# Building the transposed one-hot on VectorE from receivers spread over 64 partitions

## What is computed

```python
h   = relu(layernorm(x))
cat = concatenate((h[src], h[dst], edge_attr), axis=-1)
msg = relu(cat @ W1 + b1)
aggr = segment_sum(msg, dst, num_segments=12500)
out = x + layernorm(aggr + h, gamma, beta)
```

## Time and profile before

| what | us |
|---|---|
| median of three executions | 2785.59 |
| lowest and highest of them | 2776.02, 2791.99 |
| span of the profiled execution | 1998.5 |
| mean granted TensorE clock in it | 0.922 |
| own time of the profiled execution | not given |
| first to last gather of the main stage | 77.9 to 1983.7 |

### The profile page before, as it was taken

The page is one execution under the profiler, slowest core; times in us unless marked ns, Lnnn a source line. Parts: engine busy times, 40 slices in busy tenths (PEclk is TensorE's granted clock), DMA queues, the critical chain, the costliest instruction groups (busy, mean ns, idle before and its releaser), DMA issues.

```text
span 1998.5 us, 51574 instructions
## 1 busy us (share of the span) xinstructions
PE 1675.0 (84%) x13397; PEld 1619.2 (81%) x13397; DVE 847.0 (42%) x2958; ACT 832.9 (42%) x1853; POOL 1501.5 (75%) x1579
## 2 busy tenths in 40 slices
PE   5788889888897888888798788888888888888886
PEld 5688888788887887888787788887888778878786
DVE  7534444444344443444444343343333344334434
ACT  5544444444444444444443343343343334334333
POOL 7777777777777777777777777777777777777775
PEclk9798988898899899899899998999899899999988
DMA  9544444444444444454444444444444444444442
GB/s 267 164 126 120 125 123 125 122 135 114 131 123 122 120 132 125 114 138 121 122 135 111 123 129 117 114 128 122 113 130 115 120 118 130 116 123 125 110 129 74
DMA packets 208223, 252.43 MB, mean 126 GB/s; under 512 B 43789, under 2 KB 132341, under 8 KB 208197
## 3 DMA queue, kind: packets, MB, share of 16 engines
q1 hardware_dynamic: 136756, 139.76, 23.9%
q0 software_dynamic: 50048, 102.60, 20.6%
q10 hardware_dynamic: 21392, 9.77, 1.7%
HBM read 229.38 MB, written 22.59 MB: 126 GB/s over the span
## 4 chain that ended last, share of the span: by engine, by line
POOL 37%; issue 25%; DMA 16%; PE 14%; DVEq 4%; DVE 2%; POOLq 1%; ACT 0%; ACTq 0%; SPq 0%
POOL a_rows L523 34%; DMA a_rows<-table_a,picks 15%; PE ps_pre L683 4%; PE ps_pre L684 4%; DVEq L1209 3%; POOL aggr L486 2%; PE ps_edge L664 2%; PE ps_hot L671 2%; PE ps_sum L694 1%; PE ps_fin L694 1%; DVE msg L1205 1%; POOLq L530 0%; PE ps_sum L701 0%; DVEq L1202 0%; DVE e_norm L1237 0%
## 5 line engine op out<-in xcount | busy, mean ns | idle before, releaser
L523 POOL DMA_INDIRECT a_rows<-table_a,picks x1516 | 1445.1, 953 | 464.5 <-issue 417.8
L906 ACT ACTIVATE msg<-msg 128x512 f32<-128x512 f32 x391 | 246.4, 630 | 1037.8 <-DVE msg L1205 1029.6
L1205 DVE TENSOR_TENSOR msg<-ps_pre,a_rows 128x512 f32<-128x512 f32 x391 | 270.5, 692 | 927.5 <-DMA a_rows<-table_a,picks 643.4
L683 PE MATMUL ps_pre<-w_c,edge_cols 128*128 128x128 f32 x3128 | 650.9, 292 | 0.0
L684 PE MATMUL ps_pre<-b_win,onehot_cols 128*128 128x128 f32 x3128 | 645.3, 290 | 0.0
L683 PEld LDWEIGHTS ps_pre<-w_c,edge_cols 128*128 128x128 f32 x3128 | 522.3, 210 | 0.0
L684 PEld LDWEIGHTS ps_pre<-b_win,onehot_cols 128*128 128x128 f32 x3128 | 517.8, 208 | 0.0
L671 PE MATMUL ps_hot<-ident,onehot 128*128 128x128 f32 x1564 | 262.7, 295 | 11.2 <-DVE onehot L1186 11.2
L694 PE MATMUL ps_sum<-onehot,msg 128*128 128x64 f32 x1568 | 207.3, 276 | 72.4 <-ACT msg L906 69.0
L694 PEld LDWEIGHTS ps_sum<-onehot,msg 128*128 128x128 f32 x1568 | 196.6, 197 | 82.6 <-ACT msg L906 78.4
L664 PE MATMUL ps_edge<-ident,edges 128*128 128x128 f32 x1564 | 259.0, 292 | 1.5 <-ACT dst_f L819 1.4
(11 more groups left out here) (123 smaller groups left out, 1062.8 us busy)
## 6 DMA issues: line engine op xcount, KB each, us to landing
edges<-in_edge_attr SPq DMA_DIRECT2D x391, 256.0 KB
a_rows<-table_a,picks POOLq DMA_INDIRECT x1516
b_win<-table_b SPq DMA_DIRECT2D x391, 32.0 KB
out<-out_rows SPq DMA_DIRECT2D x97, 64.0 KB
table_b<-b_rows ACTq DMA_DIRECT2D x96, 64.0 KB
x_all<-in_x SPq DMA_DIRECT2D x13, 448.0 KB, 5.8
table_a<-a_out SPq DMA_DIRECT2D x13, 448.0 KB, 4.0
table_early<-e_rows ACTq DMA_DIRECT2D x48, 64.0 KB
```

Of the source, the lines that this page charges most:

```text
L523: pool.indirect_dma_start(a_rows[:, u, k, :], None, table_a[:, :], bass.IndirectOffsetOnAxis(ap=picks[:, u, k:k + 1], axis=0),).then_inc(s ...
L683: pe.matmul(to, edge_cols[:, u % 2, k * P:(k + 1) * P], w_c[:, :], start=True, stop=False)
L906: act.activation(msg[:, u % 2, :, :], msg[:, u % 2, :, :], ACT.Relu).then_inc(s_msg, 1)
L1205: dve.tensor_tensor(msg[:, u % 2, :, :].rearrange("p k f -> p (k f)"), ps_pre[u % 2][:, :], a_rows[:, u, :, :].rearrange("p k f -> p (k f) ...
```

## The change

The one-hot with nodes on the partitions is no longer made by transposing. SyncE loads the 512 receivers of the group, as int32, to each of 64 partitions (`dst_win`, a DMA that reads the same 2 KB of `dst` 64 times). VectorE (`hot_columns`) compares them with base + partition number, held as one column of `base_all`, and writes fp32 ones and zeros to `onehot_cols[0:64]`. Its input is read with a step of four words, since edge p*4+k belongs at column k*128+p. The four transposes of the one-hot on TensorE and the eviction on ScalarE go. The product with the window has 64 rows of contraction where it had 128, so the unused rows need no zeros and three memsets go. `count` (for `one_hot`) and the zero (for `clear`) are read from PSUM, in the bank that the transposes used. `dst_win` shares its place with buffers of the first stage, so SyncE starts the main stage when all of `table_a` is stored.

```diff
+        space = sb("space", [P, 4 * CHUNK * H])
+        dst_win = space[0:WIN, 0:UNROLL * GROUP].bitcast(I32).rearrange("w (u e) -> w u e", u=UNROLL)
...
+        ps_count, ps_zero = ps_hot[0][:, 0:WIN], ps_hot[0][:, WIN:WIN + 1]
...
                     if past(i, 1):
                         sp.wait_ge(s_edge_turned, g - UNROLL + 1)
+                        sp.wait_ge(s_hot_cols, g - UNROLL + 1)
                     sp.dma_start(edges[:, u, :], group_rows(start_of(i, u))).then_inc(s_edges[u], 16)
+                    start = start_of(i, u)
+                    sp.dma_start(dst_win[:, u, :],
+                                 dst[bass.ds(start, GROUP)].rearrange("(o e) -> o e", o=1).to_broadcast([WIN, GROUP])
+                                 ).then_inc(s_dst_win[u], 16)
...
-                sp.wait_ge(s_zero, 1)
+                for par in range(2):
+                    sp.wait_ge(s_a_stored[par], (CHUNKS // 2) * 16)
+                sp.wait_ge(s_b_first, 1)
...
+            pool.iota(part[:, :], pattern=[[0, 1]], base=0, channel_multiplier=1,
...
-                    pe.wait_ge(s_hot, g + 1)
-                    if past(g, 2):
-                        pe.wait_ge(s_hot_cols, g - 1)
-                    for k in range(SUB):
-                        mm = pe.transpose(ps_hot[u % 2][:, k * P:(k + 1) * P], onehot[:, u, k, :], ident[:, :])
-                    mm.then_inc(s_hot_turned, 1)
...
-                        mm = pe.matmul(to, onehot_cols[:, u % 2, k * P:(k + 1) * P], b_win[:, u, :],
+                        mm = pe.matmul(to, onehot_cols[0:WIN, u % 2, k * P:(k + 1) * P], b_win[0:WIN, u, :],
...
-                    act.wait_ge(s_hot_turned, g + 1)
-                    act.activation(onehot_cols[:, u % 2, :], ps_hot[u % 2][:, :], ACT.Copy).then_inc(s_hot_cols, 1)
...
-            dve.memset(zeros[:, :], 0.0)
-            dve.memset(b_win[:, :, :], 0.0)
-            dve.memset(onehot[:, :, :, :], 0.0).then_inc(s_zero, 1)
...
-                        count[:, 0:WIN].unsqueeze(1).to_broadcast([P, SUB, WIN]),
+                        ps_count.unsqueeze(1).to_broadcast([P, SUB, WIN]),
...
+                def hot_columns(i, u):
+                    g = i * UNROLL + u
+                    dve.wait_ge(s_dst_win[u], (i + 1) * 16)
+                    if past(g, 2):
+                        dve.wait_ge(s_pre, g - 1)
+                    dve.tensor_scalar(onehot_cols[0:WIN, u % 2, :].rearrange("w (k p) -> w k p", k=SUB),
+                                      dst_win[:, u, :].rearrange("w (p k) -> w k p", k=SUB),
+                                      base_all[0:WIN, bass.ds(g, 1)], None, ALU.is_equal).then_inc(s_hot_cols, 1)
...
-                    dve.tensor_copy(aggr[:, bass.ds((j + AHEAD) * P, P)], zeros[:, :])
+                    dve.tensor_copy(aggr[:, bass.ds((j + AHEAD) * P, P)], ps_zero.to_broadcast([P, P]))
...
                             one_hot(*after(i, u, 2))
+                        if not (last and u == groups - 1):
+                            hot_columns(*after(i, u, 1))
```

More of the change, by code:

```diff
@@ L106, in build @@
         ones = sb("ones", [P, P])
-        zeros = sb("zeros", [P, P])
+        part = sb("part", [P, 1])
         eps = sb("eps", [P, 1])
@@ L116, in build @@
         flag = sb("flag", [1, 1], I32)
-        centred = sb("centred", [P, 2, CHUNK, H])
+        space = sb("space", [P, 4 * CHUNK * H])
+        centred = space[:, 0:2 * CHUNK * H].rearrange("p (a b f) -> p a b f", a=2, b=CHUNK)
+        h_cols = space[:, 2 * CHUNK * H:].rearrange("p (a b n) -> p a b n", a=2, b=CHUNK)
+        dst_win = space[0:WIN, 0:UNROLL * GROUP].bitcast(I32).rearrange("w (u e) -> w u e", u=UNROLL)
         mean_all = sb("mean_all", [P, BLOCKS])
-        h_cols = sb("h_cols", [P, 2, CHUNK, P])
         a_out = sb("a_out", [P, 2, CHUNK, H])
@@ L219, in build @@
         s_b_stored = sem("s_b_stored")
-        s_zero = sem("s_zero")
         s_gate_pool = sem("s_gate_pool")
@@ L231, in build @@
         s_edge_turned = sem("s_edge_turned")
-        s_hot_turned = sem("s_hot_turned")
+        s_dst_win = [sem(f"s_dst_win{u}") for u in range(UNROLL)]
+        s_count_kept = sem("s_count_kept")
         s_edge_cols = sem("s_edge_cols")
@@ L473, in _ @@
                       allow_small_or_imprecise_dtypes=True).then_inc(s_const, 1)
+            pool.iota(part[:, :], pattern=[[0, 1]], base=0, channel_multiplier=1,
+                      allow_small_or_imprecise_dtypes=True).then_inc(s_const, 1)
             pool.memset(eps[:, :], EPS).then_inc(s_const, 1)
-            pool.wait_ge(s_const, 4)
+            pool.wait_ge(s_const, 5)
             pool.affine_select(out=ident[:, :], in_=ident[:, :], compare_op=ALU.not_equal, fill=1.0,
@@ L563, in _ @@
         def _(pe):
-            pe.wait_ge(s_const, 5)
+            pe.wait_ge(s_const, 6)
             def turn_ids(a, q):
@@ L689, in sums @@
                     g = i * UNROLL + u
+                    pe.wait_ge(s_hot, g + 1)
                     pe.wait_ge(s_msg, g + 1)
@@ L780, in _ @@
         def _(act):
-            act.wait_ge(s_const, 5)
+            act.wait_ge(s_const, 6)
             def deviate_chunk(c):
@@ L1097, in _ @@
             ins.then_inc(s_range, 1)
-            dve.wait_ge(s_const, 5)
+            dve.wait_ge(s_const, 6)
             dve.wait_ge(s_range, 2)
@@ L1123, in _ @@
             crooked = dve.value_load(flag[0:1, 0:1], min_val=0, max_val=ID_ROWS)
-            dve.wait_ge(s_zero, 1)
             dve.wait_ge(s_pad, 2)
@@ L1272, in _ @@
                 mask()
+                dve.tensor_copy(ps_count, count[:, 0:WIN])
+                dve.memset(ps_zero, 0.0).then_inc(s_count_kept, 1)
                 dve.tensor_tensor(dst_f[:, :, :], dst_f[:, :, :],
@@ L1278, in _ @@
                 dve.wait_ge(s_rel, 2)
+                dve.tensor_scalar(base_all[:, :], base_all[:, :], part[:, 0:1], None, ALU.add).then_inc(s_rel, 1)
+                dve.wait_ge(s_count_kept, 1)
                 one_hot(0, 0)
                 one_hot(0, 1)
+                dve.wait_ge(s_rel, 3)
+                hot_columns(0, 0)
                 def rounds(s, early):
```

## The result

| | before | changed |
|---|---|---|
| median of four executions, us | 2782.5 | 3455.2 |
| lowest and highest | 2776.0, 2792.0 | 3401.9, 3467.6 |

The ratio is 1.2297 with an interval of 1.2228 to 1.2366: 23% slower. The direction was the forecast one, the size lies 540 us above the upper end of the range. The profiled execution of the changed kernel took 3443.98 us and its span is 3442.2 us, so here nothing lies outside the instructions.

What follows compares the result with a forecast made beforehand. The prediction took the gathers' pace on GpSimd, 1.249 us each, as the bound. Terms -14.0 + 40.2 + 20.1 = +46.3 us on 2785.6 gave 2831.9 us, some 1.7% slower, range 2757 to 2915.

Steps and rivals of the forecast that it cites:

- The product with the window has 64 rows: TensorE's product with the window of `table_b`: contraction over 64 rows instead of 128, given no cost in the sum.
- The cover that the prediction named for TensorE: TensorE's work per group hides behind the gathers' pace unless a group costs it over 4.87 us.
- TensorE's savings worth nothing: Removing 262.7 us of TensorE transposes and 229.5 us of ScalarE evictions gains nothing, as the gathers set the pace.
- The hold of the gathers: `hot_columns` on VectorE delays GpSimd's gathers: 40.2 us at their start plus 20.1 us past their middle.
- 20.1 forecast: Delay at a gather's second critical moment, somewhat past its middle: half of the range from nothing to a full 40.2 us.
- H: Part of `hot_columns` in which data stream, put at 507 ns; bounds 271 and 1014 ns.
- the prediction's formula: Gather delay per VectorE instruction at one critical moment: H x H/(2P), with P the gathers' pace of 1249 ns.
- the first moment: Critical moment at a gather's start, where `hot_columns` was to cost 102.9 ns x 391 = 40.2 us.
- The 14.0 us for `one_hot` and `clear`: Gathers' excess over their median, saved by moving the second input of `one_hot` to PSUM: minus 14.0 us, bounds 0 and minus 20.1.
- A constant outside the instructions: The 787.1 us by which the profiled span falls short of the median time stay unchanged; called the weakest premise.
- executions without the profiler are bound otherwise: Rival: loop really lasts 2786 us, TensorE binding at its lower clock; at least 262.7 us come off, 2523 us; chance 0.11.
- Landings, SyncE's queue, the tail: Added receiver loads of 51 MB may land some tenths late, within four groups of slack: nothing; the tail stays.

Runs made afterwards that it cites:

- session 1: Follow-up runs timed together, the unchanged kernel before taking 2000.15 us; the kernel before with only the 64-row product took 2216.5 us, ratio 1.1105.
- session 5: Last follow-up runs timed together, the kernel before taking 2817.9 us; the kernel before with only the 64-row product took 3079.1 us, ratio 1.0909.
- grouped form: Changed kernel, 64 rows kept, each group's four Wc products run before its four window products: 2046.2 us, ratio 1.0230; later 2787.8 us, ratio 0.9889.
- form with 128 rows: Changed kernel with the window product contracting over 128 rows, rows 64 to 127 zeroed once: 2047.9 us, ratio 1.0238; later 2774.6 us, ratio 0.9831.
- session 4: Kernel before, unchanged, 2821.1 us, timed beside three variants of the changed kernel: 128 rows, and that with a tensor_tensor or dense-input `hot_columns`.
- four changes a group: Changed kernel with the order of the two products reversed in every second sub-group, so row count changes four times, not eight: 2428.2 us.

## Why the prediction was wrong, step by step

- **The step that failed**: "The product with the window has 64 rows", which stood in the change and had no line in the sum; its cost was put at nothing without a reason. The cover that the prediction named for TensorE ("gone only where a group costs TensorE over 4.87 us") was the right test, but the group was never costed with the new product. The runs show 0.20 us for each change of row count at the upper level and 0.29 at the lower, eight a group: 11% alone (session 1) and 9% (session 5). In the changed kernel TensorE works 3311 us behind the first 77.9, which is 8.47 us a group against the 4.87. The Trainium skill ("TensorE: Matmul & The Clock Gate", Part 3) says that a weight load is pulled ahead of matmuls in flight when it goes to other rows of the array or to the background weight buffer, and in its list of what overlaps it names only the other rows; under "Why this matters for your kernels" it says that a matmul with few rows costs the time of a full one. The last rule agrees with the 1.06 and 1.16 us of the grouped form. The list the runs contradict: loads of 128 rows behind 128 go to the same rows and ran 0.11 us ahead of their matmul. Only where 64 rows met 128, with rows 0 to 63 in common, did the overlap go. Why it goes there no run shows.
- **TensorE's savings worth nothing**: right where the row counts don't alternate and wrong in sign where they do. In session 1 the form with 128 rows has all the savings and takes what the gathers give. In the changed kernel four transposes put back raise the clock from 0.523 to 0.758 and shorten the run by some 380 us, to 3074. The kernel before with the same eight changes, its own transposes and evictions and none of the new loads and comparisons, comes to nearly the same, 3079 us at 0.756. What in TensorE's stream decides the level isn't settled: its share of busy time doesn't rank the kernels (97% at a clock of 0.52, 96% at 0.975, 79% at 0.70).
- **The hold of the gathers**: right. Where the gathers bind, 46.3 us were forecast and 47.3 measured (form with 128 rows); the total of 1491 us was forecast, 1492.9 measured. I split the lengthening in that trace, by taking each gather's length less 0.944 us and adding it up: gathers that began while `hot_columns` ran have 39.4 us in all (40.2 forecast for that moment), those during which it began 19.9 us (20.1 forecast), nearly all of it where it began 0.2 to 0.5 us into the gather; all others have 2.5 us. The length was 679 ns, not 778: the step of four words costs VectorE less than ScalarE's rows suggested (679 - 483 = 196 ns for 512 elements), so H was nearer 407 than 507 ns, for which the prediction's formula gives 25.9 us at the first moment; the 39.4 measured ask for a hold of about 0.50 us (an estimate by the same formula). The trace of the form with 128 rows shows it directly, with its gathers sorted by how far into `hot_columns` they begin: in the first 0.07 us they lose nothing, then as much as is left up to about 0.56 us (0.38 us on average at 0.14 to 0.21), and after that nothing again. So the hold lasts some 0.49 us of the 0.68. The two misses cancel, and the 20.1 was a midpoint between nothing and full, so that the sum came out within 1 us is in part luck. By the Trainium skill ("SBUF — State Buffer", Who interferes with whom) the hold lasts the whole instruction; with the forecast 778 ns the prediction gave that rule 142 us; with the measured 679 the same formula gives 108, and the runs showed about 60. The same section has tensor_tensor without such a mode, and the form with it and its second input in PSUM lost nothing (1434.3 us), which agrees.
- **The 14.0 us for `one_hot` and `clear`**: right in sign, too large. `count` in SBUF costs 7 us more across two sessions (4.5 us in the gathers). With neither source of holds the gathers come to 1434.3, 10.8 us below before.
- **"A constant outside the instructions"**: wrong, as the prediction feared. Span and time agree within 2 us in every execution looked at where the trace was taken beside the times. The trace of before, with a span of 1998.5 us, a clock of 0.922 and 232 GB/s at the start, is like those of the sessions of 2000 us, so it must have been taken in that condition and its times in the other. The rival "executions without the profiler are bound otherwise" had right that the time lies in the loop. It was wrong that TensorE's group would then be the bound (busy for 70% in session 4) and in its gain of at least 262.7 us: with the row counts repaired the change brought 1.7%, 48 of 2822 us.
- **Landings, SyncE's queue, the tail**: nothing seen to matter where the gathers bind.

## What to carry to other kernels

Put matmuls with the same number of contraction rows one behind another, or pad to the same number with zeros set once: in these fp32 products 64 rows saved nothing over 128, and alternating them took 1.9 times as long at the upper level and 1.7 times at the lower. Before taking work off an engine that isn't the bound, cost what remains there in its new form at both levels of the clock. And when a profile's own time and the times beside it disagree, find out first which conditions each was taken under; a rank of kernels may turn round between them (the form with 128 rows, 2.4% slower in one, was 1.7% faster in the other).

## What the runs showed of the hardware that was not expected

- Changing between 64 and 128 rows of contraction: 0.42 us a product against 0.22 at the upper level, 0.72 against 0.43 at the lower.
- With TensorE busy for 97 to 98% the clock stayed at the lower level for nearly the whole run (0.520 to 0.523 on average in two sessions, 0.545 to 0.601 in a third), while other kernels had 0.67 to 0.98. Busy time alone doesn't tell which: with 64 rows in the kernel before TensorE was busy for 96% at 0.975, with four changes a group for 96% at 0.666, and grouped in session 5 for 79% at 0.696.
- A gather that begins during the tensor_scalar of 679 ns is held until about 0.56 us into it, and not at all in its first 0.07 us (form with 128 rows, session 1: 39.4 us over 241 gathers).
- The kernel before takes 2000 or about 2800 us, each repeatable within a session, on the same chip at different times. In the second condition the first loads run at 126 GB/s instead of 232. What sets it, and which event VectorE then waits for, stays open.
- In that condition the form that spares the gathers is the slower one: with `hot_columns` of 676 ns 2774.6 us, with 1057 ns 2799.7 us, though its gathers are 69 us shorter in total (1433.1 against 1502.4); they wait 838 us for `picks` against 700. That the longer VectorE instruction is the cause is a reading that no run tests.
